# Moving the histogram of the last pair's sources from slots 46 to 113 to slots 150 to 217 in a two-layer graph network

## The reference

```python
h = jnp.maximum(_layernorm(x, axis=-1), 0.0)
# relational layer: bases (8,512,512), w_comp (32,8), 40000 edges, x is (1250,512)
weight = jnp.einsum('rb,bio->rio', w_comp, bases)
h_rel = jnp.einsum('ni,rio->rno', h, weight)
x = x + jax.ops.segment_sum(h_rel[etype, src] * edge_weight, dst, num_segments=1250) + h_bias
h = jnp.maximum(_layernorm(x, axis=-1), 0.0)
# graph convolution with self loops
row = jnp.concatenate([src, loops]); col = jnp.concatenate([dst, loops])
deg = jax.ops.segment_sum(jnp.ones(row.shape[0]), row, num_segments=1250)
dis = jax.lax.rsqrt(deg)
out = jax.ops.segment_sum((dis[row] * dis[col])[:, None] * (h @ W.T + b)[row], col, num_segments=1250)
x = x + relu(out)
```

## Time and profile before

| | |
|---|---|
| median of 3 runs | 622.63 us (617.65 to 623.02) |
| the profiled execution | 618.07 us |
| span of its instructions | 616.3 us |
| PE busy | 492.8 us, 80% |
| DVE busy | 348.0 us, 56% |
| POOL busy | 355.8 us, 58% |

### The profile page before, as it was taken

The page is one execution under the profiler, slowest core; times in us unless marked ns, Lnnn a source line. Parts: engine busy times, 40 slices in busy tenths (PEclk is TensorE's granted clock), DMA queues, the critical chain, the costliest instruction groups (busy, mean ns, idle before and its releaser), DMA issues.

```text
span 616.3 us, 16046 instructions
## 1 busy us (share of the span) xinstructions
PE 492.8 (80%) x5902; PEld 314.3 (51%) x5902; DVE 348.0 (56%) x972; ACT 152.8 (25%) x272; POOL 355.8 (58%) x473
## 2 busy tenths in 40 slices
PE   2031346498889989999999999899989998999983
PEld 1020344365556655666665666566656565555530
DVE  8798037885875556773665555654566423232036
ACT  3393225542221002221132220220223101122020
POOL 3333526885675676776674775767767777740000
PEclk9565757598998999999999999999999999999985
DMA  9896965556686588787685886887877878855006
GB/s 280 318 360 211 391 171 145 160 161 186 183 270 197 169 260 238 199 267 236 184 272 147 253 263 186 250 252 216 275 208 230 274 235 250 238 163 154 0 9 162
DMA packets 53429, 132.84 MB, mean 216 GB/s; under 512 B 12173, under 2 KB 18174, under 8 KB 53350
## 3 DMA queue, kind: packets, MB, share of 16 engines
q0 software_dynamic: 27040, 99.60, 53.7%
q1 hardware_dynamic: 25356, 30.99, 16.0%
q10 hardware_dynamic: 954, 1.13, 0.6%
HBM read 120.58 MB, written 11.10 MB: 214 GB/s over the span
## 4 chain that ended last, share of the span: by engine, by line
PE 55%; DVE 14%; DMA 11%; issue 6%; ACT 4%; POOL 4%; SPq 3%; ACTq 1%; DVEq 0%
PE PS L1647 24%; PE PS L1625 17%; DMA gath<-rows_layer,srcs 7%; PE PS L1688 6%; PE PS L1667 4%; POOL gath L772 4%; DMA types<-types_by_slot 2%; SPq L629 2%; DVE zt L1284 2%; ACT room_b L891 2%; DVE room_b L1284 1%; DMA edge_records<-room_c 1%; DVE room_b L1322 1%; DMA w1t<-edge_records,w1t 1%; PE PS L1631 1%
## 5 line engine op out<-in xcount | busy, mean ns | idle before, releaser
L772 POOL DMA_INDIRECT gath<-rows_layer,srcs x335 | 339.4, 1013 | 171.7 <-issue 88.3
L1625 PE MATMUL PS<-sel,gath 128*128 128x48 f16 (+7 forms) x4020 | 313.5, 206 | 39.2 <-issue 12.8
L1625 PEld LDWEIGHTS PS<-sel,gath 128*128 128x128 f16 x4020 | 243.8, 102 | 162.0 <-issue 68.5
L1647 PE MATMUL PS<-room_b,zt 128*128 128x512 f16 x480 | 162.4, 385 | 1.0 <-DVE sel L1206 0.8
L1647 PE MATMUL PS<-room_b 128*128 128x512 f16 (+1 forms) x480 | 150.5, 382 | 1.1 <-DMA gath<-rows_layer,srcs 1.1
L1631 PE MATMUL PS<-oh_ad,gath 128*128 128x30 bf16 (+7 forms) x335 | 64.5, 193 | 0.0
L1688 PE MATMUL PS<-u_t,room_c 128*128 128x512 f16 (+2 forms) x200 | 58.6, 403 | 4.9 <-issue 2.5
L1200 DVE TENSOR_TENSOR masks<-iota_n,dloc 128x24 bf16<-128x24 f32 (+12 forms) x92 | 17.7, 193 | 77.3 <-issue 43.0
L1647 PEld LDWEIGHTS PS<-room_b 128*128 128x128 f16 (+1 forms) x480 | 47.5, 104 | 14.7 <-DMA gath<-rows_layer,srcs 1.3
L832 ACT CAST val<-val_f 128x64 f16<-128x64 f32 x42 | 11.0, 261 | 170.8 <-DVE val_f L1157 170.8
L1647 PEld LDWEIGHTS PS<-room_b,zt 128*128 128x128 f16 x480 | 45.1, 99 | 5.7 <-issue 1.1
(11 more groups left out here) (224 smaller groups left out, 424.9 us busy)
## 6 DMA issues: line engine op xcount, KB each, us to landing
room_b<-in_L_gnn_bases_dram SPq DMA_DIRECT2D x8, 1024.0 KB, 10.0
gath<-rows_layer,srcs POOLq DMA_INDIRECT x335
types<-types_by_slot SPq DMA_DIRECT2D x168, 16.0 KB
x_t<-x_base SPq DMA_DIRECT2D x19, 128.0 KB
u_t<-in_x_dram SPq DMA_DIRECT2D x9, 256.0 KB, 6.4
x_base<-u_t SPq DMA_DIRECT2D x9, 256.0 KB
x_layer<-x_t SPq DMA_DIRECT2D x18, 128.0 KB
gath<-x_layer SPq DMA_DIRECT2D x18, 128.0 KB, 2.7
```

The costliest lines, as they stand in the source:

```text
L772: pool.indirect_dma_start(out=gath[:, s % UN, :], out_offset=None, in_=tab0_d[:, :], in_offset=bass.IndirectOffsetOnAxis(ap=srcs[:, s:s + ...
L1625: mm(there, gath[:, s % UN, D * t + P * f:D * t + P * (f + 1)], sel_parts[:, here, k, 0:NB * w, u], start=first and t == 0 and u == 1, sto ...
L1647: last = mm(PS[0:r, PBANK[q], :], zt[q % 2][:, t, f, b, 0:r], base_hl[:, b, u, f, :], start=(m == 0), stop=(m == NM - 1))
```

## The change

The base slot of the histogram goes from 46 to 150. Everything else of the program stays.

```diff
-        HIST_AT = 46
+        HIST_AT = 150
         STEPS[HIST_AT].append(("hprep", 0))
         for k in range(NHIST):
             STEPS[HIST_AT + 4 + 12 * k].append(("hones", k))
             STEPS[HIST_AT + 7 + 12 * k].append(("hist", k))
```

## The result

The median of 20 runs after is 623.75 us (620.4 to 626.36), that of 20 runs of the kernel before, taken beside them, 619.73 us (617.6 to 623.02). The ratio is 1.0059, 95% interval 1.0042 to 1.0077: 3.7 us (2.6 to 4.8) slower, by ratio times 619.7. The profiled execution after has a span of 619.8 us against 616.3.

A forecast was written before the change was run, and what follows sets the result against it. PE and POOL's gathers were taken to bound the kernel by turns. Late cost 11.55 us less early gain 6.3 us gave +5.2 us, which on the median 622.63 made 627.8 us (chance 46%), own range 624 to 630.5 us.

The forecast's parts named there:

- the early gain: Slots 46 to 150: moving the histogram away gives back 1.8 + 0.35 + 2.0 + 1.7 + 0.45 = 6.3 us.
- slots 181 to 184: Late stretch: `hones 2` ahead of `x1 4` makes flush 12 late, and PE loses 1.4 us waiting for it.
- the four terms for them: Early: flush wait at slot 48, 1.8 us; first sum, 0.35; waits at slot 65, 2.0; slow clock after, 1.7.
- The wait at slot 156: Preparation and `hones 0` ahead of flush 10 start it 4.0 us later; PE loses 3.8 us.
- The clock behind it: After PE's long wait at slot 156 the granted clock falls, costing 1.2 us.
- rival (a): The clock holds in the late stretch: +2.8 us, 625.4 us; chance 18%.
- `proj 4`: Slot 193: `proj 4` must wait on the shared bank for DVE's read-out of sum 3, 0.6 us.
- `turn 5`: Slot 217: `turn 5` stands behind sum 5 and DVE's read-out, 3.0 us later with sum 5 included.
- The clock there: After the two waits at slot 217 the granted clock falls, costing 1.2 us.
- (b): The gather ring takes up the stalls of slots 156 and 184: -1.2 us, 621.4 us; chance 15%.
- (c): The early gain stops at gather 82, only 3.6 us come back: +7.9 us, 630.5 us; chance 16%.
- (d): DVE's small 32-bit instructions hold up POOL's gathers, adding the preparation's 3.35 us: +8.5 us, 631.1 us; chance 5%.

The follow-up runs named there:

- e1: The kernel before with the histogram left out (preparation, one-hot rows, sums and their waits); 609.3 us, ratio to before 0.9845.
- e5: The kernel before without the histogram, plus six groups of three DVE instructions with two SBUF inputs; 614.94 us, ratio to before 0.9943.
- e6: The kernel before without the histogram, plus six groups of three one-input reductions over as many elements; 610.12 us, ratio to before 0.9857.
- e12: The kernel before without the histogram, plus six groups of three two-input DVE instructions at slots 50 to 110; 611.76 us, ratio to before 0.9889.
- e7: The kernel before with preparation moved from slot 46 to 43, `hones 1` 62 to 67, `hist 1` 65 to 71; 613.13 us, ratio to before 0.9918.
- e4: The kernel after with 20 unused matmuls put into PE's wait at slot 155; 622.05 us, ratio to before 1.0038.
- e3: The kernel after with `hones 5` moved from slot 214 to 208 and `hist 5` from 217 to 211; 620.4 us, ratio to before 1.0015.
- e10: The kernel after with the late histogram's parts placed by hand away from flushes, layer norms and turns; 613.9 us, ratio to before 0.9907.
- e9: The kernel after with `hones 2` moved from slot 178 to 186 and `hist 2` from 181 to 189; 622.98 us, ratio to before 1.006.
- e2: The kernel after with preparation moved from slot 150 to 143, `hones 0` 154 to 156, `hist 0` 157 to 162; 618.01 us, ratio to before 0.9981.

## Why the prediction was right or wrong

The direction held, and both the forecast and the ratio of 1.0059 lie within 1%. The time, 627.8, was 4.05 us too high, and 623.75 lies just under the forecast's own range of 624 to 630.5. That range was too narrow: the bounds given for the terms add up to 620.2 to 633. Three steps failed: the base, the term put at nothing in the early gain, and the cause at slots 181 to 184.

**The base.** 2.9 of the 4.05 us are this: I put the difference on the median of three runs, 622.63, when the profiled execution already stood at 618.07; the median of 20 runs is 619.73. The text had both numbers and took the worse one. The other 1.15 us is the difference itself, +5.2 against the medians' +4.0. Against the true base the forecast said 8.1 us slower, twice what was measured.

**That the difference came out so near is in part luck.** Both sides were too small by about as much: in the traces the early stretch gave 7.9 us where I had 6.3, and the late one took 13.3 where I had 11.55.

**The early gain, 6.3 us, was too small: 9.6 by e1, 7.9 in the pair of traces.** The step "sums 2 and 3 lie behind gather 82, where PE waits for gathers anyway: nothing" failed. In the pair of traces slots 46 to 75 give 5.9 us, as much as the four terms for them (1.8 + 0.35 + 2.0 + 1.7); slots 76 to 100 give 0.9, where I had nothing, and slots 101 to 150 give 1.1, where I had 0.45. The step looked only at what the sums take on PE. The row that told of more stood in the earlier trace rows: gather 82 took 2.37 us, the other four rows of the group 0.94 or 0.95. It ran beside `hones 2`. PE's wait for gathers, which I took as cover, is the very chain that the one-hot rows lengthen (e5 and e6 show it, e12 makes it likely here). The three large terms held (e7: 5.1 against 5.5).

**The wait at slot 156, 3.8 us, held.** The flush begins at 306.32. In the kernel before, with the trace's shift of 9.50 at slot 150, it would have begun at 302.48: 3.84 later, against my 4.0, and PE is 3.84 us late as well (307.19 against 312.85 - 9.50). The bank wasn't 0.17 us old before, as I had it: in both traces PE begins 0.87 us behind the flush. The profile puts 5.17 us down to it, since PE also comes to it earlier than before.

**The clock behind it, 1.2 us, was 1.9** (the 5.77 us of slots 151 to 156 less 3.84 of wait, by the traces; 2.0 by e4). It fell, as the sum had it and rival (a) had not. The Trainium skill's rule that I weighed it by ("TensorE: Matmul & The Clock Gate", "What's actually happening", activity releases the throttle) agrees: with PE kept busy, the clock held.

**Slots 181 to 184, 1.4 us, took 2.1, and by another cause.** Flush 12 is late, as the step said: it begins at 351.75, which is 2.3 us later than 352.63 less the shift of 3.21 at slot 180. But PE doesn't meet it first, and finds the bank ready (slot 184 took 4.11 us against 4.33 before). The step that failed is "sums 1 and 2 themselves fall where PE waits for gathers". `look 25` is the next user of the shared bank after sum 2, and DVE reads sum 2 out only behind `hones 2`, the layer norm of `x1 4` and the selection matrices. PE waits for that in all four traces with pair 2 at 178 and 181 and in none of the others. In the kernel after the wait shows as 0.71 us only, because PE had already lost 1.72 us at slot 181 to a late gather; in e3, which had no such wait, it is 2.14. That gather was used 5.8 us after its issue (340.54), but e10's, with no one-hot rows near it, was used 5.7 us after (335.34 to 341.06), so it is scatter and not the rows. Whether the held gathers would cost as much here without the read-out stays open: e5, with a group of two-input instructions at slot 176 and no sums, loses 2.7 us in these four slots to waits for gathers.

**`proj 4`, 0.6 us, held** (0.47 of wait at 371.15, 0.7 in the table). **`turn 5`, 3.0 us, was 2.6**, by the queue that I wrote down: the read-out ended at 404.53, where I had 404.6. **The clock there, 1.2 us, did not come** in the profiled execution, nor in e4, but it did in e9 and e2, where slots 218 and 219 took 1.5 to 1.7 us more than in the kernel after. So it is a term of chance and not a fixed one. What I put at nothing, slots 201 to 217 and 219 to 334, took 1.6 us together; `hones 4` and `hones 5` stand beside gathers of 1.35 and about 1.0 us, but no run took these apart, and among the traces these stretches scatter by as much.

**The rivals.** (b), the ring takes up the stalls, is refuted by the gather at 311.90, which waits 4.88 us for PE, and by gather 175, whose 3.98 us did not shrink. (c), the gain stops at gather 82, fails on slot 150. (d) was wrong for the preparation: the gathers beside it keep to their pace (296.24 to 300.00, 0.95 us each). But its mechanism, DVE against POOL's gathers, was at work all the same, in the instructions with two large inputs, at both places. It is part of the early gain as well as of the late cost, and so partly cancels in the difference.

## What to carry to other kernels

A step that is off the critical path costs what it delays in its neighbours' queues, so it belongs behind a flush, a layer norm or a shared bank's next user and not ahead of them: the same histogram cost 3.7 to 3.8 us well placed and 9.6 to 13.3 badly placed. An indirect gather that takes 2.4 us where its neighbours take 0.95 points to a DVE instruction with two SBUF inputs beside it, and "the engine waits for gathers there anyway" is then no cover but the path. Put a difference of a few tenths of a per cent on the profiled execution or on many runs, not on the median of three.

## What the runs showed of the hardware

Three DVE instructions with two SBUF inputs, 2.16 us together, stretched the longest gather beside them from 0.95 to between 1.19 and 1.78 us (e5, six groups), to 2.37 in the kernel before and to 2.56 in the kernel after, there with the layer norm's instructions right behind; three reductions of 2.13 us together over as many elements did not (e6), nor did a flush with one input from SBUF and one from PSUM. Six such groups cost 6.1 us of the kernel's time (e5 over e1), put where PE keeps up with the gathers; the whole histogram, well placed, costs 3.7. And behind nearly the same pair of waits (0.42 and 1.55, or 0.54 and 1.55 us) the granted clock held at 1.00 in one execution and had a mean of 0.68 over the next 5.3 us in another; it held behind a longer pair too (0.67 and 1.73, e4).
